# Early-fusion kernel, opening stage: where the side-row copies are issued, how many PSUM banks image 1's projections use, and the order of the first bands, gray values and table loads

## The reference, cut to what matters

```python
gray  = einsum('bchw,c->bhw', x, (0.2989, 0.587, 0.114))      # x: 8 images, 3 x 256 x 256
edges = conv(gray, scharr, padding='SAME')                    # two 3x3 filters
h = concat([abs(edges).sum(filters) / 2, txt], axis=1)        # 8 x 384 x 256
h = h + attn0(layernorm(h))       # 16 heads of 16, two key kinds, softmax, projections Q, K, K', V, O
h = h + ffn0(layernorm(h))        # fp4-quantised feed-forward
h = h + attn1(layernorm(h))       # attention over 64 anchors
h = h + moe(layernorm(h))         # one shared and 8 routed experts
```

## Time and profile before

| | us |
|---|---|
| median of 3 runs (1808.31 to 1811.04) | 1810.0 |
| the profiled execution, its own time | 1810.65 |
| its span in the profile | 1808.9 |
| where the first ring starts and ends in it | 73.06 and 127.20 |
| mean granted TensorE clock, share of full | 0.992 |

### The profile page before, as it was taken

How to read it: one execution, slowest core, us unless ns; L and a number is a source line. 1 busy time by engine, 2 the same in 40 slices (tenths; PEclk the granted TensorE clock), 3 DMA queues, 4 the chain that set the end, 5 groups by cost and what they waited for, 6 DMA issues and landing times.

```text
span 1808.9 us, 29077 instructions
## 1 busy us (share of the span) xinstructions
PE 1731.5 (96%) x9935; PEld 1111.2 (61%) x9935; DVE 999.9 (55%) x2010; ACT 680.6 (38%) x1293; POOL 409.2 (23%) x415
## 2 busy tenths in 40 slices
PE   6889899999999998999999999999999999999997
PEld 3334344344444435777755665666767679999997
DVE  6597877778778897888865444443211111222221
ACT  2126656566566686454533322333111111111110
POOL 2202021120211013988721221110211211010000
PEclk9999999999999999999999999999999999999999
DMA  5742542525425202000083000000000003432211
GB/s 182 132 93 75 74 81 41 96 52 93 80 41 102 68 2 74 1 0 0 1 318 87 0 0 0 0 1 1 36 26 21 32 20 114 173 107 105 102 32 34
DMA packets 112051, 112.83 MB, mean 62 GB/s; under 512 B 11509, under 2 KB 104535, under 8 KB 111960
## 3 DMA queue, kind: packets, MB, share of 16 engines
q1 hardware_dynamic: 98616, 83.21, 20.4%
q10 hardware_dynamic: 9696, 18.97, 2.9%
q0 software_dynamic: 3648, 9.46, 1.4%
HBM read 78.51 MB, written 32.93 MB: 62 GB/s over the span
## 4 chain that ended last, share of the span: by engine, by line
PE 85%; DVE 7%; ACT 2%; issue 2%; ACTq 1%; DMA 1%; SPq 0%; DVEq 0%; POOL 0%; POOLq 0%
PE ps_e L2282 11%; PE ps_e L2215 9%; PE ps_a L652 7%; PE ps_m L1715 6%; PE ps_a L606 6%; PE ps_a L641 6%; PE ps_e L2291 5%; PE ps_m L1858 5%; PE ps_e L2224 5%; PE ps_m L1786 4%; PE ps_m L1816 4%; PE ps_a L577 3%; PE ps_m L1731 3%; DVE mx L1005 2%; PE ps_a L728 1%
## 5 line engine op out<-in xcount | busy, mean ns | idle before, releaser
L1005 DVE TENSOR_REDUCE mx<-ps_a 128x1 f32<-128x384 f32 x672 | 333.1, 549 | 45.9 <-PE ps_a L606 44.3
L860 ACT ACTIVATE prob<-ps_a 128x768 f32<-128x768 f32 (+1 forms) x512 | 306.1, 651 | 97.5 <-PE ps_a L641 96.4
L606 PE MATMUL ps_a<-w,qs 96*128 96x384 bf16 x672 | 212.5, 333 | 5.0 <-DVE mx L1005 3.0
L641 PE MATMUL ps_a<-qs,w 100*128 100x384 bf16 x768 | 206.3, 330 | 5.9 <-issue 3.0
L2282 PEld LDWEIGHTS ps_e<-xTr,w 128*128 128x128 f32 x1792 | 204.4, 192 | 2.2 <-issue 0.8
L2282 PE MATMUL ps_e<-xTr,w 128*128 128x128 f32 x1792 | 204.7, 275 | 0.6 <-DVE xTr L2458 0.6
L652 PE MATMUL ps_a<-prob,vp 128*32 128x384 f32 x1536 | 163.5, 498 | 0.0
L606 PEld LDWEIGHTS ps_a<-w,qs 96*128 96x128 bf16 x672 | 63.7, 97 | 154.7 <-DVE mx L1005 80.3
L2215 PE MATMUL ps_e<-xT_all,w 128*128 x448 | 145.7, 486 | 0.0
L2347 ACT ACTIVATE gel_r<-ps_e 128x512 f32<-128x512 f32 x56 | 33.4, 597 | 280.1 <-PE ps_e L2282 280.1
L1715 PE MATMUL ps_m<-w 128*128 128x352 f32 x384 | 122.3, 462 | 2.2 <-ACT w L1892 1.2
(11 more groups left out here) (273 smaller groups left out, 2649.8 us busy)
## 6 DMA issues: line engine op xcount, KB each, us to landing
w<-parts_dram SPq DMA_DIRECT2D x192, 96.0 KB, 5.3
w<-in_L_ffn_W_dram ACTq DMA_DIRECT2D x18, 1024.0 KB, 8.4
parts_dram<-w SPq DMA_DIRECT2D x24, 576.0 KB, 3.5
qs<-parts_dram SPq DMA_DIRECT2D x96, 96.0 KB, 4.0
prob<-in_x_dram SPq DMA_DIRECT2D x24, 256.0 KB, 3.6
w<-in_L_ffn_W_dram SPq DMA_DIRECT2D x6, 1024.0 KB, 12.6
grouped_x<-empty_row SPq DMA_DIRECT2D x1, 4352.0 KB, 23.8
grouped_h<-empty_row SPq DMA_DIRECT2D x1, 4240.5 KB, 33.4
```

The costliest lines, as they stand in the source:

```text
L606: mm = pe.matmul(ps[:, r % 3, 0:T], qs[0:NS, b, u // 2, t * P:(t + 1) * P], ks[0:NS, b, u % 2, u // 2], start=True, stop=True)
L641: mm = pe.matmul(ps[:, scores_at(v, more) + t, 0:T], ks[0:NS + 4, b, kp, hh, t * P:(t + 1) * P], qs[0:NS + 4, b, hh], start=True, stop=True)
L860: act.activation(prob[:, g % 2, j, ts.start:ts.stop], ps[:, at + ts.start:at + ts.stop, 0:T], ACT.Exp).then_inc(exp_done.sem, 1)
L1005: dve.tensor_reduce(at, ps[:, r % 3, 0:T], AX.X, ALU.max).then_inc(ring_free.sem, 1)
```

## The change

Five edits, all in the opening:

1. `sides(i)` moves from ACT's stream to SP's. Image 0's stands behind the load of image 1, image i-1's behind the load of image i for i from 2 to 5, and those of images 5, 6 and 7 behind both halves of image 0's stacks. The load of image 7 now stands between the first and the second store of image 0's parts.
2. ACT begins with a root of a constant, so that the table of the root is loaded first; all waits on `root_done` count one more.
3. Image 0's gray values stand behind the first band instead of the third, and each piece of image 0's edges waits for its own band.
4. Image 1's turned inputs and projections use banks 3 and 7 in turn; a step waits for the step two before it.
5. `store_parts(1)` stands ahead of `kinds(1)` on SP.

```diff
+    PREPARE_BANKS = (3, 7)
@@ sync
+            def sides(i):        # body as on ACT before, sp.wait_ge / sp.dma_start
             image(1)
+            sp.wait_ge(borders.sem, 3)
+            sides(0)
             sp.dma_start(al[:, 0:1], ...)
-            for i in range(2, B):
+            for i in range(2, B - 1):
                 image(i)
+                if i < BESIDE + 1:
+                    sides(i - 1)
             sp.wait_ge(kinds_made.sem, 4)
             kinds(0)
-            store_parts(0)
+            store_parts(0, (0,))
+            image(B - 1)
+            store_parts(0, (1, 2))
             stacks(0, 0, 0)
             stacks(0, 0, 1)
-
-            sp.wait_ge(edges_done.sem, edges_done.at(HELD, 0))
-            kinds(1)
+            for i in range(BESIDE, B):
+                sides(i)
             for m in range(3):
                 sp.wait_ge(stack_in[1][m].sem, stack_in[1][m].at(1, 0))
             store_parts(1)
+            sp.wait_ge(edges_done.sem, edges_done.at(HELD, 0))
+            kinds(1)
             stacks(1, 1, 0)
@@ tensor
-                    if i == 0 and kx == 0:
-                        pe.wait_ge(bands_done.sem, 9 * (f + 1))
+                    if i == 0:
+                        pe.wait_ge(bands_done.sem, 3 * (n + 1))
...
                 if r < len(PREPARE):
-                    last = in_bank3(PREPARE[r][0], 1, PREPARE[r][1], last)
+                    step, n = PREPARE[r]
+                    if r >= 2:
+                        signal, count = freed[r - 2]
+                        pe.wait_ge(signal.sem, signal.at(1, count))
+                    do, signal = STEPS[step]
+                    do(1, n, PREPARE_BANKS[r % 2])
+                    freed.append((signal, n + 1))
@@ scalar
-            act.wait_ge(borders.sem, 3)
-            sides(0)
-            sides(1)
+            act.wait_ge(borders.sem, 1)
+            act.activation(rstd[:, 0:1], eps[:], ACT.Sqrt, bias=eps[:]).then_inc(root_done.sem, 1)
             magnitudes(0)
+            act.wait_ge(root_done.sem, 1)
...
-            sides(2)
...
-                if n < 5:
-                    sides(n + 2)
...
-            sides(7)
@@ vector
-                if f == 0:
-                    dve.wait_ge(borders.sem, 3)
-                    make_gray(0)
+                    if f == 0 and kx == 0:
+                        dve.wait_ge(borders.sem, 3)
+                        make_gray(0)
```

More of the change, by code:

```diff
@@ L386, in _, with store_parts @@
         def _(sp):
-            def store_parts(i):
-                for m in range(3):
+            def store_parts(i, kinds_of=range(3)):
+                for m in kinds_of:
                     sp.wait_ge(parts_done.sem, parts_done.at(i, KC * (m + 1)))
@@ L449, in image @@
                                  ).then_inc(pix_in[i % 2].sem, 16)
+            def sides(i):
+                gray, side = gray_of(i), side_of(i)
+                sp.wait_ge(gray_step.sem, gray_step.at(i, 3))
+                sp.wait_ge(side_zero.sem, 2 if i < 2 else 4)
+                for a, row in ((1, gray[0:1, 1, 0:IMG]), (0, gray[P - 1:P, 0, 0:IMG])):
+                    shifted = bass.AP(row.tensor, row.offset, [list(row.ap[0]), [1, 3], [1, IMG]])
+                    for f in range(2):
+                        to = f * UPPER + 3 * (1 - a)
+                        sp.dma_start(side[to:to + 3, 1 - a], shifted).then_inc(side_in[i].sem, 16)
             sp.dma_start(taps[:], scharr.rearrange("f o a b -> (f o a b)").partition_broadcast(P)
@@ L768, in _ @@
             pe.wait_ge(v_done.sem, v_done.at(0, 2))
-            last = None
+            freed = []
             for r in range(FIRST):
@@ L934, in _ @@
                     if step == "inputs":
-                        copy_inputs(1, n)
+                        copy_inputs(1, n, PREPARE_BANKS[r % 2])
                     else:
-                        high_part(1, n)
+                        high_part(1, n, PREPARE_BANKS[r % 2])
                 i = edges_before(r, 0)
@@ L1167, in inverses @@
             def inverses(n, first, end):
-                dve.wait_ge(root_done.sem, n + 1)
+                dve.wait_ge(root_done.sem, n + 2)
                 tiles = slice(first * TT, end * TT)
@@ L1229, in _ @@
                 if r < len(PREPARE) and PREPARE[r][0] == "project":
-                    low_parts(1, PREPARE[r][1])
+                    low_parts(1, PREPARE[r][1], PREPARE_BANKS[r % 2])
                 if r == 2:
@@ L1243, in _ @@
             dve.memset(F.floor, FLOOR).then_inc(w4_zero.sem, 1)
-            dve.wait_ge(root_done.sem, 5)
+            dve.wait_ge(root_done.sem, 6)
             tiles = slice(0, (B - 1) * TT)
```

## The result

| | before | after |
|---|---|---|
| median, us | 1810.06 (4 runs, 1808.31 to 1811.04) | 1796.66 (4 runs, 1795.44 to 1796.97) |
| the profiled execution, us | 1810.65 | 1795.44 |
| its span, us | 1808.9 | 1793.7 |
| first ring starts, ends | 73.06, 127.20 | 60.80, 110.71 |

The ratio is 0.9921, with a 95% interval of 0.991 to 0.9933: 13.4 us faster, a small gain (0.7% by the medians) but clear of the scatter. The profiled execution of after is the shortest of its four.

What follows compares the result with a forecast made beforehand. PE bounds the kernel, losing time in the opening to late ACT work and a one-bank round trip. Savings 3.1 + 4.0 + 2.7 + 4.1 = 13.9 us from the 1810.0 median give 1796.1, stated as 1796.0; range 1791 to 1801 (8 in 10).

Steps and rivals of the forecast that it cites:

- to image 1's edges: Opening up to image 1's edges: with ACT free they start at 21.8 instead of 24.93, saving 3.1 us.
- image 2's edges to image 4's: Image 4's edges on PE: their wait for image 2's magnitudes on ACT goes, saving 4.0 us.
- image 4's edges to the ring: Image 4's edges: the low clock goes with the wait, 8.02 us becoming 5.31, saving 2.7 us.
- the landing of image 0's side rows: Before image 0's corner piece: the SP call's last DMA lands about 18.0, judged by alpha's 7.1 us.
- early case: Image 0's side rows land by the corner piece's old start, 17.06; the first term is then 4.0, not 3.1.
- more than that: Opening rival: high clock in image 1's edges (1.5), early side rows (0.9), tighter projections (about 1); about 1793; chance 0.27.
- less: Opening rival: PE waits anew in image 0's projections, clock falls, banks give half; saving about 10, 1800; chance 0.18.
- I leave its 12.5 us as they are: Image 0's projections up to image 2's edges: PE sets the pace, 12.5 us unchanged, edges starting at 44.2.
- The two banks: Ring entries 2 to 7: period 1.9 us instead of 2.73, saving 4.1 us net, bounds 0 to 5.6.
- Table, gray values, stores: Opening: earlier gray values and reordered stores give nothing; the second table load's move from before the root gives nothing.
- The slow-SP rival: SP calls of x us become serial; ring from 45 + 4x, even at 8.0; chance 0.04 still faster, 0.03 slower.
- Signs named beforehand: New profile: one early table load, edges near 21.8, corner piece 17 to 18.5, ring near 63, later ring 34.8.

Runs made afterwards that it cites:

- e5: Kernel before with only the side rows moved to SP at the changed kernel's places, against the kernel before: 1799.47 us, ratio 0.9934.
- e4: Changed kernel with image 0's gray values back behind the third band: 1795.04 us, ratio 0.9918 to the kernel before.
- e8: The changed kernel measured once more, nothing altered, as yardstick for later variants: 1796.39 us, ratio 0.9922 to the kernel before.
- e2: Changed kernel with image 1's projections back in one bank, each step behind the one before: 1799.32 us, ratio 0.9943 to the kernel before.
- e3: Changed kernel without the early root on ACT, its semaphore only counted up: 1796.61 us, ratio 0.9927 to the kernel before.
- e6: Changed kernel with spare copies making each SP side call of images 0 to 4 eight DMAs, 5.4 us: 1804.28 us, ratio 0.9963 to the kernel before.
- e7: Changed kernel with spare copies making each SP side call of images 0 to 4 twelve DMAs, 8.1 us: 1815.41 us, ratio 1.0026 to the kernel before.
- e11: Changed kernel with SP loading image i+2 before image i's side rows, and image 0's side rows on ACT: 1793.17 us, ratio 0.9905 to the kernel before.
- e9: Changed kernel with SP loading image i+2 before issuing image i's side rows: 1793.79 us, ratio 0.9909 to the kernel before.

## Why the prediction was right, point by point

**The size.** 1796.0 was forecast and 1796.66 measured. The terms do not all agree that well. In the two profiled executions the ring ends 16.5 us earlier (127.20 to 110.71), where the sum had 13.9.

| step | in the sum | in the profile | how |
|---|---|---|---|
| to image 1's edges | 3.1 | 4.3 | 24.77 to 20.50 |
| from there to the projections | 0 | 0.9 | 10.01 to 9.11 |
| projections | 0 | 0.5 | 12.48 to 11.97 |
| image 2's edges to image 4's | 4.0 | 4.1 | 16.80 to 12.70 |
| image 4's edges to the ring | 2.7 | 2.5 | 9.00 to 6.52 |
| entries 0 to 7 | 4.1 | 4.2 | 19.35 to 15.11 |
| the rest of the ring | 0 | 0 | 34.80 |

The starts are those of the timeline; for image 1's edges the chain, from which the prediction read 24.93, gives 0.16 us more than the timeline's 24.77.

**The step that was mis-sized** is the landing of image 0's side rows, "about 18.0". They had landed at 16.32, 3.8 us after SP had issued the last. The 7.1 us of alpha was a poor stand-in. That is 1.7 us, of which 1.3 reached image 1's edges (20.50, not 21.8). It is one execution: in the five profiles of such a call on SP where the piece waits, it starts at 16.19 to 17.24, four of them ahead of the old start, 17.06, which the prediction had as its early case.

**The projections.** They took 8.01 us instead of 9.70. The rival "more than that" had this gain, about 1 us, but for a reason that the runs refute: that they get tighter without ACT's DMAs. e5 has no DMAs on ACT either, and PE of e5 shows:

```profile
28.86 9.61 PE L595 MATMUL ps_a<-w,wT 128*128 128x384 f32 x24 [0.96 <-ACT w L841]
```

What goes with the time is the granted clock (1.00 is the upper of its two levels, 2.4 GHz; a lower mean has part of the stretch at 1.2): 0.82 over the projections before (34.78 to 44.30), 0.83 in e5 (28.86 to 38.40), and 1.00 in after (29.61 to 37.60). At the same time the wait that "less" named came about: image 5's gray values stood on DVE, their planes late by a call, and PE waited 1.27 us. The two nearly cancel, which is why "I leave its 12.5 us as they are" came out at 11.97. e4 and e5 show the effect plainly: e4's projections start 1.6 us before those of after (28.01), its ring only 0.8; e5's take 1.6 us more than those of after, but its V projection then meets no wait and its ring starts at 60.3.

**Where 16.5 became 13.4.** The profiled executions differ by 15.2 us, and stand 0.6 above the median of before and 1.2 under that of after, which makes 13.4. The other 1.3 are lost behind the ring: 0.5 by 700 us, where after is 16.0 ahead, and 0.8 at the start of the routed experts, shown below. From the ring's end to the execution's end the thirteen profiles take 1682.8 to 1685.7 us, the kernel before 1683.5 and after 1684.7. The edits change no instruction there, so this looks like scatter; with one profile for each, a part that goes with a kernel cannot be excluded. Windows of the routed experts' start before, then after (the clock is the third number from the end):

```profile
1494.00:1502.40 8.40, 7.41 (x64) 7.22 (x64) 0.96 (x2) 1.14 (x2) 1.37 (x2) 1.00 1.03 374
```

```profile
1478.00:1487.30 9.30, 8.88 (x65) 8.89 (x66) 0.97 (x2) 0.60 (x1) 1.39 (x2) 0.82 1.03 366
```

The same 64 products take 8.88 instead of 7.41 us, at a granted clock of 0.82. The kernel before then waits 0.63 us for a DMA, which after does not, so 0.8 of the difference is lost. So the good fit to 1796.0 is in part two misses that cancel: the opening gave 2.6 us more than the sum, and the medians 3.1 less than the profile's opening. The second comparison of the same two kernels (e8) has 14.5 between the medians.

**The two banks** were right in mechanism and in the total: 4.2 in the profile, and e2 takes it back. The parts of that total were not: the period is 1.79 us, PE's own 1.8 and not the 1.9 of DVE that the sum used, and the gain of the shorter periods is in part given back at the end, where PE waits 1.38 us for DVE in front of image 5's edges (75.91; before 0.77). **Table, gray values, stores** were taken at nothing, and e3, e4 and e5 agree.

**The slow-SP rival** was the right danger. Its condition did not arise, since a call took 2.71 us. At x = 5.4 and 8.1 its formula 45 + 4x gives ring starts of 66.6 and 77.4, where 69.1 and 80.1 were measured: the slope held, and the constant was 2.6 us too low. The slope held by luck. The formula follows image 6's gray values, at 27 + 4x or 48.6 and 59.4; they start at 50.70 (e6) and 64.05 (e7), which is five calls' growth, not four. But the last gray values that PE waits for are image 5's, which start at 42.55 and 53.49, four calls' growth apart, and the ring starts 26.6 us behind them in both. The balance turns at 7.0 us, not at 8.0: the constant takes it to 7.4, and the rest is that e7's median is 4.5 us above the kernel before where its ring ends 2.9 late.

**Signs named beforehand** that held: a gap on PE before the corner piece that ends with a DMA, one table load before the first exponential, no wait of image 4's edges, the first stack issued at 48.88 (forecast 47.8) with no wait of PE at the ring, the later part of the ring still 34.8, and what follows shifted as a whole to within 0.5 us up to the routed experts. Early against their forecast were the corner piece (16.32, its band was 17 to 18.5), image 1's edges (20.50, not 21.8) and the ring (60.80, not 63).

## What to carry to other kernels

Where an engine's stream is in order, count the DMAs it issues as work of that engine, and look for their cost not at one wait but at every place where something of its is taken late; the place moves when other things change. Before such issues go to another queue, write down what stands behind them there: loads that compute waits for go ahead of small copies that have slack (2 to 3 us here), and the number of calls ahead of the load that is waited for is the slope at which a longer issue comes back (four calls, 4.1 here). Check which load that is, since another one has another slope. A saving read in two single profiles should be set against the scatter of the part that the change does not touch.

## What the runs showed of the hardware

- A table load does not wait for what its activation waits for: it ran at 0.82 where the activation came at 18.19 (e3).
- Small copies within SBUF cost SP about what they cost ACT to issue (mostly 0.63 to 0.68 us each; ACT's median is 0.67), and two and three times as many cost it in proportion (e6, e7). Single ones cost more: up to 3.06 on ACT, 1.28 on SP (the first of e7).
- In the same kernel image 1's edges took 6.11 us once, at a granted clock of 0.82 from 20.5 to 24.9, and 5.32 once, at 1.00 (after and e8). The projections, the same work in all kernels, took 8.01 us in after, e8 and e11, granted 1.00 from 24.9 to 32.8, and 9.43 and 9.61 in e9 and e5, granted 0.78 there. Shortly before the projections PE had waited 2.18 us in e9 and 0.77 in e11, but in e5 nothing beyond the 0.96 right in front of them, and the runs do not say what decides.
- DVE's two gray products took 1.42 us where POOL was idle (after, 36.94) and 2.19 us where it worked on the parts; POOL's cast beside them took 0.96 us instead of 0.50. No run varies this alone. DVE of e11:

```profile
34.37 2.19 DVE L1172 SCALAR_TENSOR_TENSOR w<-prob,w 128x512 f32<-128x512 f32 x2
```

and POOL of e11 at that time:

```profile
34.10 1.01 POOL L546 TENSOR_TENSOR w<-w 128x384 bf16<-128x384 f32 x1
35.05 0.96 POOL L544 CAST w<-w 128x384 bf16<-128x384 f32 x1
```
